# S4D long convolution on one core: undivided sums and state products, another order in every engine's slot, and Y's last table rows made by two engines

## The chip, the cores and the metric

One core of a Trainium2 chip. The metric is the device time of one execution in microseconds; lower is better.

## The reference

For each of 128 channels `h`, a real kernel `K[h, 0:2048]` is made of 64 complex exponentials, and every one of 64 sequences of 2048 samples is convolved with it causally; then come the skip term, the mask by length and the residual:

```python
A = -jnp.exp(log_A_real) + 1j * A_imag
dtA = A * dt[:, None]
P = dtA[:, :, None] * jnp.arange(length, dtype=jnp.float32)
Cs = Cc * (jnp.exp(dtA) - 1.0) / A
K = 2.0 * jnp.einsum('hn,hnl->hl', Cs, jnp.exp(P)).real
...
y = jnp.fft.irfft(u_f * k_f, n=n)[..., :Lq]
y = y + u_m * D[:, None]
return y * mask[:, None, :]          # and the result is x + this
```

x is float32 of 64 x 128 x 2048, so 64 MiB are read and 64 MiB written.

## The kernel before

No FFT is used. A sequence is cut into eight chunks of 256 samples, two halves of the sequence set side by side on the 128 partitions (64 sequences each). For one channel:

- TensorE transposes x in eight blocks of 128x128 (`turn_x`, parity 0 into `xt_even`, parity 1 into `xt_odd`), and the table E of the channel in two (`turn_e`).
- *Sums:* `even_sums` and `odd_sums`, three products of 448 columns each, bring each chunk into the state space (complex, 64 modes: real parts on one half of the partitions, imaginary on the other), in the PSUM bank `v`.
- *Scan:* VectorE carries the states from chunk to chunk: `pairs`, `fours`, `sixth`, `odds`, each as two dependent operations (the first into `mid`, the second into `v`). Multiplying by i needs the halves of the partitions swapped, which ScalarE does (`turn_odds`, `turn_pairs`, `turn_evens`, all into `turned`). The first operations of each are `fours_turned` and, after the change, `pairs_turned` and `odds_turned`.
- *Inside a chunk:* `toep_even` (three products each) and `toep_odd`, with the kernel's first 256 values as a Toeplitz matrix `traw` that SyncE loads with a DMA from `krows` in DRAM (`load_t`).
- *From the states:* `from_state`, twelve products of 256 columns with the scaled states `zhi`, `zlo` and the table F, into the bank `y`.
- *Choice and residual:* VectorE's `choose` copies `y` under the mask over x, in two halves of 512 columns; SyncE stores the result.

Products are fp32r with numbers split in a high part and a rest: ScalarE rounds the high part (`x_high`, `x_odd`, `e_high`, `f_high`, `t_high`, `z_high`), and VectorE or GpSimd subtracts it (`x_low`, `e_low`, `z_low` on VectorE; `f_low`, `t_low`, `odd_low` on GpSimd). GpSimd also makes E and F of a channel: two products of tables (16 x 16 each) and their `difference`.

The order on every engine is written out by hand: each has a `slot(g, j)` which handles stages of several channels (`here`, `one` ahead, `two` ahead, `three` ahead, `back`). `groups` runs it for channels 0 to 11 written out, for 12 to 119 in a hardware loop of 18 rounds of six, and for 120 to 127 written out. In TensorE's slot the even sums of the next channel come first, then the odd half of x two channels ahead, the odd sums, four Toeplitz steps with `turn_e` in the middle, and the products from the states, with the even half of x three channels ahead after the first six. Engines meet at semaphores, each counted up by one operation and waited for with the channel's number.

Ahead of the slots lies a prologue of some 60 us: VectorE and ScalarE compute powers of exp(dt A); GpSimd builds the table B by doubling (`level`, 1, 2, 4, 8 rows of 16), VectorE builds Y and then X, which needs the square root of a complex number (the norm on ScalarE, `m0`). TensorE transposes each four rows in the order of `STEPS` through three PSUM banks (`pro`), and ScalarE copies them to their place (`take`). B and X are doubled by a copy first (`double_b`, `double_x`). Then TensorE makes K (`k_fenced`, `k_rest`), which goes to `krows`. `keep_warm` are transposes without use.

## Time and profile before

| | |
|---|---|
| median of 3 runs | 887.85 us (887.10 to 889.97) |
| profiled execution | 887.13 us, span 885.3 us, mean granted clock 0.99 |
| busy | PE 829.4, VectorE (DVE) 758.5, ScalarE (ACT) 669.0, GpSimd (POOL) 605.6 us |
| DMA | 152.71 MB, 172 GB/s over the span |
| chain that ended last | PE 89%, DVE 4%, ACT 2%, DMA 2% |

A record of a row begins with its start from the start of the span and its duration, in us; the engine, the line, the operation, output<-input and their shapes follow, and in brackets the idle time of the engine ahead of it and who ended it. Records of one engine can overlap by the length of its pipeline.

### The profile page before, as it was taken

What the parts mean: (1) busy time and instruction counts of PE and PEld (TensorE: products, weight loads), DVE (VectorE), ACT (ScalarE), POOL (GpSimd) and SP (SyncE); (2) the same over time, 40 slices, a digit from 0 to 9 for tenths busy, and PEclk for the clock granted to TensorE, in tenths of its full rate; (3) what the DMA queues carried; (4) which work ended last, traced back from release to release, by engine and by line L of the source; (5) the groups of instructions that cost most, each with busy time, mean ns of one, the idle gap of its engine ahead of it and who ended that gap; (6) DMA issues with size and microseconds to landing.
All of it is one profiled execution on the core that took longest, in us unless ns stands there. A gap on an engine that the chain in (4) does not pass through costs nothing.

```text
span 885.3 us, 22927 instructions
## 1 busy us (share of the span) xinstructions
PE 829.4 (94%) x6281; PEld 788.1 (89%) x6281; DVE 758.5 (86%) x2041; ACT 669.0 (76%) x1720; POOL 605.6 (68%) x843
## 2 busy tenths in 40 slices
PE   0579999999999999999999999999999999999997
PEld 0569999999999999999999999999999999999996
DVE  7768888888888888888888888888888888888886
ACT  4567777777878787777777787878777777878784
POOL 5936767767676767676776767676767677676762
PEclk9789999999999999999999999999999999999999
DMA  5225787878877777877777778778787877778784
GB/s 104 48 61 115 175 194 177 187 186 186 186 184 190 180 191 175 190 178 192 180 187 184 185 186 182 191 180 188 178 189 179 190 181 185 184 186 186 185 191 107
DMA packets 161393, 152.71 MB, mean 172 GB/s; under 512 B 13656, under 2 KB 161240, under 8 KB 161240
## 3 DMA queue, kind: packets, MB, share of 16 engines
q1 hardware_dynamic: 161064, 152.15, 73.6%
q10 hardware_dynamic: 304, 0.26, 0.1%
q8 instruction: 11, 0.18, 0.1%
q14 instruction: 14, 0.11, 0.1%
HBM read 84.02 MB, written 67.30 MB: 171 GB/s over the span
## 4 chain that ended last, share of the span: by engine, by line
PE 89%; DVE 4%; issue 2%; ACT 2%; DMA 2%; SPq 0%; POOL 0%; DVEq 0%; ACTq 0%
PE y L1093 16%; PE y L1094 13%; PE y L1095 13%; PE y L1141 12%; PE xt_odd L1078 6%; PE xt_even L1078 6%; PE v L1093 6%; PE v L1094 6%; PE v L1095 6%; PE y L1088 2%; PE y L1089 2%; DMA xall<-in_x_dram 1%; ACT room L588 1%; PE y L1236 0%; ACT B L588 0%
## 5 line engine op out<-in xcount | busy, mean ns | idle before, releaser
L588 ACT ACTIVATE room<-v 64x192 f32<-64x192 f32 (+1 forms) x768 | 235.8, 307 | 153.3 <-DVE v L963 74.0
L963 DVE SCALAR_TENSOR_TENSOR mid<-room,RV,v 128x192 f32<-128x192 f32 (+2 forms) x512 | 183.1, 358 | 66.0 <-ACT room L588 58.9
L963 DVE SCALAR_TENSOR_TENSOR v<-v,RV,mid 128x192 f32<-128x192 f32 (+2 forms) x512 | 191.0, 373 | 38.6
L952 DVE COPY_PREDICATED xall<-mask,y 128x512 f32<-128x512 int32 x254 | 190.4, 750 | 0.5 <-issue 0.4
L1093 PE MATMUL y<-thi,uhi 128*128 128x256 f32 x511 | 175.9, 344 | 0.0
L1093 PE MATMUL y<-fhi,zhi 128*128 128x256 f32 x511 | 163.6, 320 | 12.7 <-DVE zlo L1008 1.2
L1095 PE MATMUL y<-fhi,zlo 128*128 128x256 f32 x511 | 144.3, 282 | 0.0
L1094 PE MATMUL y<-tlo,uhi 128*128 128x256 f32 x511 | 143.9, 282 | 0.0
L1094 PE MATMUL y<-flo,zhi 128*128 128x256 f32 x511 | 143.9, 282 | 0.0
L1095 PE MATMUL y<-thi,ulo 128*128 128x256 f32 x511 | 143.8, 281 | 0.0
L1141 PE MATMUL y<-traw,uod 128*128 128x128 f32 x680 | 130.5, 273 | 0.0
L1093 PEld LDWEIGHTS y<-fhi,zhi 128*128 128x128 f32 x511 | 96.7, 189 | 32.5 <-issue 32.5
L520 POOL TENSOR_TENSOR flo<-pf,fhi 128x256 fp32r<-128x256 f32 x64 | 46.6, 728 | 100.1 <-ACT fhi L588 100.1
L520 POOL TENSOR_TENSOR flo<-room,fhi 128x256 fp32r<-128x256 f32 x64 | 46.7, 729 | 96.2 <-ACT fhi L588 96.2
L557 POOL TENSOR_TENSOR uol<-uod,uoh 128x448 fp32r<-128x448 f32 x85 | 98.5, 1159 | 17.3 <-issue 14.1
L1141 PEld LDWEIGHTS y<-traw,uod 128*128 128x128 f32 x680 | 104.7, 190 | 0.0
L1093 PEld LDWEIGHTS y<-thi,uhi 128*128 128x128 f32 x511 | 97.4, 191 | 2.1
L1094 PEld LDWEIGHTS y<-tlo,uhi 128*128 128x128 f32 x511 | 97.8, 191 | 1.5
L1094 PEld LDWEIGHTS y<-flo,zhi 128*128 128x128 f32 x511 | 97.0, 190 | 0.0
L1095 PEld LDWEIGHTS y<-fhi,zlo 128*128 128x128 f32 x511 | 96.4, 189 | 0.0
L1095 PEld LDWEIGHTS y<-thi,ulo 128*128 128x128 f32 x511 | 96.1, 188 | 0.0
L525 POOL TENSOR_TENSOR tlo<-traw,thi 128x256 fp32r<-128x256 f32 x128 | 93.7, 732 | 0.3 <-ACT thi L588 0.3
(217 smaller groups left out, 2110.1 us busy)
## 6 DMA issues: line engine op xcount, KB each, us to landing
xall<-in_x_dram SPq DMA_DIRECT2D x256, 256.0 KB, 4.6
out_dram<-xall SPq DMA_DIRECT2D x254, 256.0 KB, 3.3
traw<-krows SPq DMA_DIRECT2D x128, 128.0 KB, 3.6
NXY<-B SPq DMA_DIRECT2D x2, 512.0 KB, 6.1
krows<-ksb SPq DMA_DIRECT2D x8, 1.0 KB, 2.2
krows<-ksb SPq DMA_DIRECT2D x8, 4.0 KB, 3.8
krows<-ksb SPq DMA_DIRECT2D x8, 11.0 KB, 4.0
out_dram<-xall SPq DMA_DIRECT2D x1, 128.0 KB, 2.5
```

The lines of the kernel that those rows point to most:

```text
L520: pool.tensor_tensor(flo[j % 2][:], pf[j % 2][:, ::-1], fhi[j % 2][:].bitcast(F32), ALU.subtract).then_inc(s_flo, 1)
L525: pool.tensor_tensor(tlo[j % 2][:], traw[j % 2][:, ::-1], thi[j % 2][:].bitcast(F32), ALU.subtract).then_inc(s_tlo, 1)
L557: pool.tensor_tensor(uol[j % 2][:], uod[j % 3][:, 0:EVERY], uoh[j % 2][:].bitcast(F32), ALU.subtract).then_inc(s_uol, 1)
L588: return act.activation(dst, src, ACT.Copy)
L952: dve.copy_predicated(xs[j][:, a:a + 512], mask[:, a:a + 512], yb[j % 2][part][:]).then_inc(s_pred, 1)
L963: return dve.scalar_tensor_tensor(out=out, in0=src, scalar=RV[:, k:k + 1, h], in1=other, op0=ALU.mult, op1=ALU.add)
L1078: mm = pe.transpose(xt[par][:, c * P:(c + 1) * P], xs[j][:, b * BLK:(b + 1) * BLK], ident[:])
L1088: pe.transpose(e_bank(j)[:, 0:P], pf[j % 2][:, 0:P], ident[:])
L1093: pe.matmul(o, a_hi, b_hi, start=start, stop=False, skip_group_check=True)
L1094: pe.matmul(o, a_hi, b_lo, start=False, stop=False, skip_group_check=True)
L1095: return pe.matmul(o, a_lo, b_hi, start=False, stop=stop, skip_group_check=True)
L1141: mm = pe.matmul(y_cols(g, j, c)[:, BLK:2 * BLK], uod[j % 3][:, b], traw[k][:, :BLK - 1:-1], start=False, stop=False, skip_group_check=True)
```

## The change

- TensorE's slot: even and odd sums of the next channel together; then all eight transposes of x two channels ahead; the products from the states undivided.
- VectorE's slot: both `choose` first; then the first operations of `odds` and of the next channel's `pairs`, then their second ones, `x_low`, `z_low`; `e_low`, `fours` and `sixth` of the next channel at the end.
- ScalarE's slot: `x_odd_high` (split off `x_odd`), `t_high` and `f_high` first; `x_high` and `x_odd` ahead of `z_high`.
- GpSimd's slot: the two table products apart, two channels ahead instead of three; `difference` last.
- SyncE: the load of x first in the slot and three channels ahead instead of four; the load of the Toeplitz matrix ahead of the store.
- Prologue: the square root right behind its squares and ahead of R's copies, an unused `Sqrt` earlier; B's last rows placed ahead of X's; the last eight rows of Y by GpSimd (four) and VectorE (four); B's last doubling by ScalarE instead of GpSimd; two more `keep_warm`; `fours` and `sixth` of channel 0 ahead of the slots.

```diff
--- before.py
+++ after.py
@@ -36,14 +36,14 @@
...
          ("B1", 12), ("B2", 12), ("Y1", 12), ("Y1", 8), ("B1", 8), ("B2", 8),
-         ("X1", 12), ("X2", 12), ("X1", 8), ("X2", 8), ("X1", 0), ("X1", 4), ("X2", 0), ("X2", 4),
-         ("B1", 0), ("B1", 4), ("B2", 0), ("B2", 4), ("Y1", 0), ("Y1", 4), ("S", 0)]
+         ("X1", 12), ("X2", 12), ("X1", 8), ("X2", 8), ("B1", 0), ("B1", 4), ("B2", 0), ("B2", 4),
+         ("X1", 0), ("X1", 4), ("X2", 0), ("X2", 4), ("Y1", 0), ("Y1", 4), ("S", 0)]
 T_K = len(STEPS)
...
 
-WARM, WARM_K = 16, 6
+WARM, WARM_B, WARM_Y = 16, 14, 4
 ROUND = 1.5 * 2.0 ** 23
...
@@ -279,10 +280,12 @@
...
-        def level(eng, link, table, turn, temps, k):
+        def level(eng, link, table, turn, temps, k, lo=0, hi=None):
 
             m = 2 ** k
-            old, new = slice(SQ - m, SQ), slice(SQ - 2 * m, SQ - m)
+            hi = m if hi is None else hi
+            old, new = slice(SQ - m + lo, SQ - m + hi), slice(SQ - 2 * m + lo, SQ - 2 * m + hi)
+            m = hi - lo
             re, im, re_new, im_new = table(old, 0), table(old, 1), table(new, 0), table(new, 1)
...
@@ -393,7 +396,7 @@
...
                 load_t(0, j)
-            tables_placed(sp, ("B2", 4))
+            tables_placed(sp, ("X2", 4))
             sp.dma_start(bsel[0:N], B1[0:N]).then_inc(s_bsel, 16)
...
@@ -403,6 +406,9 @@
...
                 early = isinstance(g, int) and g < 2
+                if exists(g, j, 3) and not (early and h + 3 < SLOTS):
+                    sp.wait_ge(s_out[(j + 3) % SLOTS], 32 * on(g, j, 3)[0])
+                    load_x(*on(g, j, 3))
                 if early and 2 <= h <= 5:
...
@@ -415,15 +421,12 @@
...
                     sp.wait_ge(s_kd_rest, 16 * 8)
+                if exists(g, j, 2):
+                    sp.wait_ge(s_intra, h + 1)
+                    load_t(*on(g, j, 2))
                 if exists(g, j, -1):
...
                     store(*on(g, j, -1))
-                if exists(g, j, 2):
-                    sp.wait_ge(s_intra, h + 1)
-                    load_t(*on(g, j, 2))
-                if exists(g, j, 4) and not (early and h + 4 < SLOTS):
-                    sp.wait_ge(s_out[(j + 4) % SLOTS], 32 * on(g, j, 4)[0])
-                    load_x(*on(g, j, 4))
             groups(sp, slot)
...
@@ -506,9 +509,9 @@
...
                 pool.wait_ge(s_nb, k)
-            late = slice(0, SQ // 2)
-            pool.tensor_copy(NB[:, late, 0, :], NB[:, late, 1, :]).then_inc(s_blate, 1)
-            pool.tensor_copy(NB[:, late, 3, :], NB[:, late, 2, :]).then_inc(s_blate, 1)
+            pool.wait_ge(s_ny, 2)
+            level(pool, link, lambda i, c: NXY[:, i, 1, c, :], (lre[:, A_POW + 3], lim[:, A_POW + 3]),
+                  [q1, q3, mag_flat, wide], 3, 0, 4).then_inc(s_ypool, 1)
             for n in range(2):
...
@@ -525,17 +528,14 @@
...
-            def table(g, j):
+            def product(g, j, which):
 
                 h = chan(g, j)
-                w1 = W1[:, 0, h, :].unsqueeze(2).broadcast_to([P, SQ, SQ])
-                w2 = W2[:, :, h].unsqueeze(2).broadcast_to([P, SQ, SQ])
-                b1 = B1[:, h, :].unsqueeze(1).broadcast_to([P, SQ, SQ])
-                b2 = B2[:, h, :].unsqueeze(1).broadcast_to([P, SQ, SQ])
-                if exists(g, j, -2):
+                w = (W1[:, 0, h, :], W2[:, :, h])[which].unsqueeze(2).broadcast_to([P, SQ, SQ])
+                b = (B1, B2)[which][:, h, :].unsqueeze(1).broadcast_to([P, SQ, SQ])
+                if which == 0 and exists(g, j, -2):
                     pool.wait_ge(s_pf, h - 1)
-                pool.tensor_tensor(tw1, w1, b1, ALU.mult).then_inc(s_gpa, 1)
-                pool.tensor_tensor(tw2, w2, b2, ALU.mult).then_inc(s_gpa, 1)
+                pool.tensor_tensor((tw1, tw2)[which], w, b, ALU.mult).then_inc(s_gpa, 1)
 
...
@@ -559,27 +559,24 @@
...
-                here, one, two, three = (g, j), on(g, j, 1), on(g, j, 2), on(g, j, 3)
-                has1, has2, has3 = exists(g, j, 1), exists(g, j, 2), exists(g, j, 3)
+                here, one, two = (g, j), on(g, j, 1), on(g, j, 2)
+                has1, has2 = exists(g, j, 1), exists(g, j, 2)
+                if has2:
+                    product(*two, 0)
                 f_low(*here)
-                if not exists(g, j, -1):
-                    t_low(*here)
-                if has2 and exists(g, j, -1):
-                    difference(*two)
                 if has1:
                     odd_low(*one)
-                if has2 and not exists(g, j, -1):
+                if has2:
+                    product(*two, 1)
+                t_low(*here)
+                if has2:
                     difference(*two)
-                if exists(g, j, -1):
-                    t_low(*here)
-                if has3:
-                    table(*three)
-
+
+            tables_placed(pool, ("X2", 4))
+            product(0, 1, 0)
+            product(0, 1, 1)
+            difference(0, 1)
             odd_low(0, 0)
-            tables_placed(pool, ("B2", 4))
-            table(0, 1)
-            difference(0, 1)
-            table(0, 2)
             groups(pool, slot)
...
@@ -594,6 +591,9 @@
...
                 copy(uod[j % 3][:], xt[1][:]).then_inc(s_uod, 1)
+
+            def x_odd_high(g, j):
+                act.wait_ge(s_tr, 2 * chan(g, j) + 2)
                 if exists(g, j, -2):
...
@@ -623,6 +623,8 @@
...
                            scale=-1.0).then_inc(s_sin, 1)
+            act.wait_ge(s_pool0, 1)
+            act.activation(one_root[:], pw[:, 0:1], ACT.Sqrt)
             act.wait_ge(s_lam, 2)
...
@@ -646,32 +648,35 @@
...
-            take(("R", 0), ("R", 1))
             act.wait_ge(s_z, 1)
...
             act.activation(sq_im, z_im, ACT.Square).then_inc(s_sq, 1)
+            act.wait_ge(s_n2, 1)
+            act.activation(m0, n2, ACT.Sqrt).then_inc(s_m0, 1)
+            take(("R", 0), ("R", 1))
             act.wait_ge(s_nb, 1)
             double_b(slice(12, 16))
-            take(("B1", 12), ("Y1", 12))
-            act.wait_ge(s_n2, 1)
-            act.activation(m0, n2, ACT.Sqrt).then_inc(s_m0, 1)
             x_high(0, 0)
             x_odd(0, 0)
-            take(("Y1", 8), ("Y1", 8))
+            take(("B1", 12), ("Y1", 12))
+            x_odd_high(0, 0)
             act.wait_ge(s_nb, 2)
             double_b(slice(8, 12))
-            take(("B1", 8), ("B2", 8))
+            take(("Y1", 8), ("B2", 8))
             act.wait_ge(s_nx, 1)
...
             take(("X1", 8), ("X2", 8))
+            act.wait_ge(s_nb, 3)
+            double_b(slice(0, SQ // 2))
+            take(("B1", 0), ("B2", 4))
             act.wait_ge(s_nx, 3)
             double_x(slice(0, SQ // 2))
-            take(("X1", 0), ("B2", 4))
+            take(("X1", 0), ("X2", 4))
             act.wait_ge(s_ny, 3)
-            tables_placed(act, ("B2", 4))
+            tables_placed(act, ("X2", 4))
             copy(b0[:, 0], B1[:, 0, :])
...
@@ -730,22 +735,24 @@
...
                 has0, has1, has2 = exists(g, j, 0), exists(g, j, 1), exists(g, j, 2)
-                three, has3 = on(g, j, 3), exists(g, j, 3)
+                if has1:
+                    x_odd_high(*one)
+                t_high(*here)
+                if has1:
+                    f_high(*one)
                 turn_evens(*here)
...
                         k_copy(j)
-                    t_high(*one)
+                if has2:
+                    x_high(*two)
+                    x_odd(*two)
                 z_high(*here)
                 if has1:
-                    f_high(*one)
                     turn_pairs(*one)
...
                     e_high(*two)
-                    x_odd(*two)
-                if has3:
-                    x_high(*three)
 
...
@@ -755,8 +762,6 @@
...
             turn_pairs(0, 0)
-            t_high(0, 0)
-            x_high(0, 2)
             groups(act, slot)
...
@@ -911,7 +916,7 @@
...
             dve.wait_ge(s_ny, 2)
-            level(dve, link, y_table, coarse[3], temps, 3).then_inc(s_ny, 1)
+            level(dve, link, y_table, coarse[3], temps, 3, 4, 8).then_inc(s_ny, 1)
 
...
@@ -963,11 +968,15 @@
...
-            def pairs(g, j):
-
-                h, z, m, w = chan(g, j), chunks(vb[j % 2]), mid[j % 2], turned[j % 2]
+            def pairs_turned(g, j):
+
+                h, z, m, w = scan(g, j)
                 dve.wait_ge(s_turn1, h + 1)
                 times(m[:], w[:, 0:3], h, 1, z[:, 2:7:2]).then_inc(s_mid1, 1)
+
+            def pairs(g, j):
+
+                h, z, m, w = scan(g, j)
                 dve.wait_ge(s_mid1, h + 1)
...
@@ -995,11 +1004,15 @@
...
-            def odds(g, j):
-
-                h, z, m, w = chan(g, j), chunks(vb[j % 2]), mid[j % 2], turned[j % 2]
+            def odds_turned(g, j):
+
+                h, z, m, w = scan(g, j)
                 dve.wait_ge(s_turn4, h + 1)
                 times(m[:], w[:, 0:3], h, 1, z[:, 3:8:2]).then_inc(s_mid4, 1)
+
+            def odds(g, j):
+
+                h, z, m, w = scan(g, j)
                 dve.wait_ge(s_mid4, h + 1)
...
@@ -1013,29 +1026,27 @@
...
                 has0, has1, has2, hasb = exists(g, j, 0), exists(g, j, 1), exists(g, j, 2), exists(g, j, -1)
-                if has1:
-                    e_low(*one)
-                fours(*here)
-                if hasb and has1:
-                    dve.wait_ge(s_y, 2 * h - 1)
-                    choose(*back, 0)
-                sixth(*here)
-                if hasb and has1:
-                    dve.wait_ge(s_y, 2 * h)
-                    choose(*back, 1)
-                odds(*here)
-                if hasb and not has1:
+                if hasb:
                     dve.wait_ge(s_y, 2 * h - 1)
...
                     choose(*back, 1)
+                odds_turned(*here)
+                if has1:
+                    pairs_turned(*one)
+                odds(*here)
                 if has1:
                     pairs(*one)
-                z_low(*here)
                 if has2:
                     x_low(*two)
+                z_low(*here)
                 if has1:
                     fours_turned(*one)
+                if has2:
+                    e_low(*two)
+                if has1:
+                    fours(*one)
+                    sixth(*one)
                 if isinstance(g, int) and g == 0 and j == 1:
...
@@ -1044,14 +1055,18 @@
...
             dve.wait_ge(s_b0, 1)
-            tables_placed(dve, ("B2", 4))
+            tables_placed(dve, ("X2", 4))
             first_table()
...
             x_low(0, 1)
+            pairs_turned(0, 0)
             pairs(0, 0)
+            e_low(0, 1)
             fours_turned(0, 0)
+            fours(0, 0)
+            sixth(0, 0)
             dve.wait_ge(s_mask, 2)
...
@@ -1062,10 +1077,12 @@
...
-            def keep_warm(n, bank):
-
+            def keep_warm(n, t):
+
+                if t >= BANKS:
+                    pe.wait_ge(s_free[t % BANKS], t // BANKS)
                 for _ in range(n):
-                    pe.transpose(bank[:, 0:P], ident[:], ident[:])
+                    pe.transpose(pro[t % BANKS][:, 0:P], ident[:], ident[:])
 
...
@@ -1160,10 +1177,10 @@
...
                     even_sums(*one)
+                    odd_sums(*one)
                 if has2:
+                    turn_x(*two, 0)
                     turn_x(*two, 1)
-                if has1:
-                    odd_sums(*one)
                 if isinstance(g, int) and g == 0 and 1 <= j <= 4:
...
@@ -1177,11 +1194,7 @@
...
                     toep_odd(*here, c)
-                for c in range(2):
-                    from_state(*here, c)
-                if exists(g, j, 3):
-                    turn_x(*on(g, j, 3), 0)
-                for c in range(2, CPH):
+                for c in range(CPH):
                     from_state(*here, c)
...
@@ -1240,7 +1253,7 @@
...
             turn_x(0, 0, 1)
-            keep_warm(WARM, pro[BANKS - 1])
+            keep_warm(WARM, STEPS.index(("B1", 12)))
             pe.wait_ge(s_bdup, 1)
...
@@ -1254,16 +1267,18 @@
...
                 turn(("X2", i), ("X2", i))
+            keep_warm(WARM_B, STEPS.index(("B1", 0)))
+            pe.wait_ge(s_bdup, 3)
+            turn(("B1", 0), ("B2", 4))
             pe.wait_ge(s_nx, 3)
...
             turn(("X2", 0), ("X2", 4))
-            pe.wait_ge(s_blate, 1)
-            turn(("B1", 0), ("B1", 4))
-            pe.wait_ge(s_blate, 2)
-            turn(("B2", 0), ("B2", 4))
+            keep_warm(WARM_Y, STEPS.index(("Y1", 0)))
+            pe.wait_ge(s_ypool, 1)
+            turn(("Y1", 0), ("Y1", 0))
             pe.wait_ge(s_ny, 3)
-            turn(("Y1", 0), ("Y1", 4))
+            turn(("Y1", 4), ("Y1", 4))
             tables_placed(pe, ("Y1", 4))
...
@@ -1274,7 +1289,6 @@
...
             turn_e(0, 1)
-            turn_x(0, 2, 0)
             tables_placed(pe, ("S", 0))
...
```

## Rows read from the trace of the kernel before

**Rows 1.** The page: busy us of each engine (share of the span) xinstructions.

```profile
PE 829.4 (94%) x6281; PEld 788.1 (89%) x6281; DVE 758.5 (86%) x2041; ACT 669.0 (76%) x1720; POOL 605.6 (68%) x843
```

**Rows 2.** Windows: stretch, length, busy time of each engine, granted clock, DMA, GB/s.

```profile
70.00:100.00 30.00, 30.00 (x242) 29.43 (x242) 24.99 (x67) 23.50 (x62) 19.45 (x27) 1.00 0.62 145
```

**Rows 3.** Timeline of TensorE (PE), a slot and a bit of the loop.

```profile
401.58 0.39 PE L1141 MATMUL y<-traw,room 128*128 128x128 f32 x2
402.07 0.36 PE L1093 MATMUL y<-fhi,zhi 128*128 128x256 f32 x1
402.26 0.28 PE L1094 MATMUL y<-flo,zhi 128*128 128x256 f32 x1
...
405.47 0.36 PE L1095 MATMUL v<-uoh,elo 128*128 128x448 f32 x1
...
408.46 0.35 PE L1093 MATMUL y<-fhi,zhi 128*128 128x256 f32 x1
```

**Rows 4.** Timeline, SyncE's queue (SPq), two channels written out near the end.

```profile
855.59 0.33 SPq L373 DMA_DIRECT2D traw<-krows  x1
...
861.87 0.33 SPq L373 DMA_DIRECT2D traw<-krows  x1
```

**Rows 5.** Timeline of VectorE (DVE), the same stretch of the loop.

```profile
406.67 0.41 DVE L963 SCALAR_TENSOR_TENSOR mid<-room,RV,v 128x192 f32<-128x192 f32 x1 [0.43 <-ACT room L588]
407.22 0.43 DVE L963 SCALAR_TENSOR_TENSOR v<-v,RV,mid 128x192 f32<-128x192 f32 x1
407.63 0.68 DVE L1008 SCALAR_TENSOR_TENSOR zlo<-v,RV,zhi 128x448 fp32r<-128x448 f32 x1
408.24 0.68 DVE L775 TENSOR_TENSOR ulo<-xt_even,uhi 128x512 fp32r<-128x512 f32 x1
408.83 0.33 DVE L963 SCALAR_TENSOR_TENSOR mid<-room,RV,v 128x128 f32<-128x128 f32 x1
409.09 0.41 DVE L775 TENSOR_TENSOR elo<-y,ehi 128x256 fp32r<-128x256 f32 x1
...
409.69 0.75 DVE L952 COPY_PREDICATED xall<-mask,y 128x512 f32<-128x512 int32 x1
```

**Rows 6.** Timeline of ScalarE (ACT), the same stretch of the loop.

```profile
405.86 0.66 ACT L588 ACTIVATE room<-v 64x192 f32<-64x192 f32 x2 [0.53 <-PE v L1095]
...
406.87 0.62 ACT L727 ACTIVATE zhi<-v,RV 128x448 fp32r<-128x448 f32 x1
...
409.16 0.55 ACT L588 ACTIVATE uoh<-xt_odd 128x448 fp32r<-128x448 f32 x1
```

**Rows 7.** The chain that ended last: start, us, what; one group of transposes.

```profile
74.88 0.44 PE xt_even L1078 x4
```

**Rows 8.** Timeline of the prologue, all engines.

```profile
19.51 0.39 ACT L588 ACTIVATE y<-lre 128x256 f32<-128x256 f32 x1 [2.14 <-DVE lre L866]
...
26.43 0.78 DVE L896 SCALAR_TENSOR_TENSOR root<-root 128x64 f32<-128x64 f32 x1 [2.25 <-ACT root L652]
...
31.21 1.28 ACT L657 ACT_TABLE_LOAD   x1
...
32.79 0.55 DVE L902 RECIPROCAL root<-root 128x64 f32<-128x64 f32 x1 [3.37 <-ACT root L657]
...
36.33 1.26 POOL L299 TENSOR_TENSOR room<-xall 128x512 f32<-128x512 f32 x1
...
36.38 1.30 DVE L908 TENSOR_TENSOR NXY<-root 128x64 f32<-128x64 f32 x1
...
46.97 1.09 ACT L588 ACTIVATE W<-v 128x512 f32<-128x512 f32 x2
...
52.89 0.46 PE L1222 MATMUL y<-B,W 64*128 64x128 f32 x2 [1.50 <-ACT W L641]
```

**Rows 9.** Timeline of GpSimd (POOL), the same stretch of the loop.

```profile
409.84 1.16 POOL L557 TENSOR_TENSOR uol<-room,uoh 128x448 fp32r<-128x448 f32 x1 [0.16 <-issue]
```

**Rows 10.** DMA issues by tile: count, KB each, median us from issue to landing.

```profile
xall<-in_x_dram SPq DMA_DIRECT2D x256, 256.0 KB, 4.6
```

More of the change, by code:

```diff
@@ L183, in s4d_kernel @@
         s_n2 = sem("s_n2")
+        s_ypool = sem("s_ypool")
         s_m0 = sem("s_m0")
```

2 lines of the change are left out of this document (1 added, 1 removed).

## The prediction

> **What bounds the kernel now.** I read the page first: TensorE is busy for 94% of the span [rows 1], so either its own work or something that it waits for sets the end. The split into windows separates the two. Between 70 and 100 us TensorE has no idle time at all [rows 2]. Later, in the loop, the timeline shows one slot (one channel) every 6.39 us: the first product from the states starts at 402.07 and the next at 408.46 [rows 3]. That stretch is not pure work. The last Toeplitz product starts at 401.58 and ends at 401.97. Its next neighbour should end 0.12 us later, as products of 256 columns do here, but ends at 402.43: TensorE stands for 0.34 us. So its own work in a slot is 6.39 - 0.34 = 6.05 us. The 0.34 us are lost 108 times in the loop (channels 12 to 119). The slots that are written out before and after it run at 861.87 - 855.59 = 6.28 us [rows 4].
>
> What ends that wait is VectorE's `z_low`, seen one slot later: it starts at 407.63 [rows 5], ends at 408.31, and TensorE's product starts at 408.46. Following it back closes a ring: the last odd sum ends at 405.47 + 0.36 = 405.83 [rows 3]; ScalarE turns the halves at 405.86 to 406.52 [rows 6]; VectorE's `pairs` start at 406.67 and 407.22, and `z_low` at 407.63 [rows 5]; then TensorE does the products from the states, one group of four transposes (0.44 us, [rows 7]) in their middle, the even sums, a second group of four between the two halves of the sums, and the odd sums. The ring is 1.80 us off TensorE (405.83 to 407.63) and 4.59 us from there to the next end of the odd sums. It is this ring, and no engine's busy share, that is 6.39 us long.
>
> **The change part by part.** *TensorE's slot.* The same instructions in another order: both halves of the sums first, then all eight transposes of the next channel, then the Toeplitz products, then the twelve products from the states undivided. Work stays at 6.05 us. In the ring, the transposes lay between `z_low` and the end of the odd sums; now they lie behind the sums, beside the work of ScalarE and VectorE. The ring loses 2 x 0.44 = 0.88 us on its TensorE side.
>
> *The other side of the ring gets longer*, since VectorE now puts its work between. From the end of the odd sums: ScalarE's turn 0.03 + 0.66 (as 405.83 to 406.52), the step to VectorE 0.15 (406.52 to 406.67), then `pairs_turned`, `odds`, `pairs` and `x_low` ahead of `z_low`. In unbroken flow VectorE starts the next instruction about 0.07 us before the last one's record ends (408.83 + 0.33 against 409.09, [rows 5]), so these take 0.41 - 0.07 = 0.34, 0.43 - 0.07 = 0.36 twice, and 0.60 (407.63 to 408.24, same width class as `x_low`). Sum 0.69 + 0.15 + 0.34 + 0.72 + 0.60 = 2.50 us against 1.80 before. The second road to `z_low` goes over ScalarE: it turns, then copies `x_high` and `x_odd` (two copies of 512 columns lie 0.49 us apart, as 1.09 - 0.60 in [rows 8]), then `z_high` 0.62 [rows 6] and the step of 0.15: 0.69 + 0.03 + 0.98 + 0.62 + 0.15 = 2.47 us. Both arrive together. New ring: 6.39 - 0.88 + (2.50 - 1.80) = 6.21 us; with the few hundredths of uncertainty of each overlap I take 6.20. That is above TensorE's 6.05, so the ring still decides and a stall of about 0.15 us remains ahead of the products from the states. Gain in the loop: 108 x 0.19 = 20.5, taken between 108 x 0.14 and 108 x 0.24.
>
> The written-out slots have the same ring at 6.28; it drops by the same 0.18 to 6.10, near the floor of 6.05. Slots 1 to 4 also hold K's products on TensorE and have no stall, so they keep their time. Some 13 slots x 0.19 = 2.5 us.
>
> *What is moved past what, and what hides it.* VectorE takes both `choose` copies at the head of the slot, behind the end of the products from the states of the channel before. They take 0.75 us each [rows 5]. The first can start at about the slot's start, so `odds_turned` can follow at 1.4 us and has to be out by 2.2, when the turned halves of the sums arrive: 0.4 us of cover are left after it. If that cover went, every further 0.1 us would cost 13 us in all. Queued behind these waits are `odds`, `pairs` and `z_low`, for which TensorE waits. ScalarE's `f_high` goes to the head of its slot and waits for the last product from the states; behind it stand `turn_evens` and `turn_odds`. It ends 0.6 us into the slot, `turn_evens` at 1.3, and the odd sums' end comes at 1.4: cover 0.1 us only, and this is the thinnest place of the ring. `f_low` on GpSimd is then done a slot early, which ends its long waits for ScalarE at no gain, as the ring did not go through it. `x_odd_high` moves to the slot's head (0.55 us, [rows 6]); GpSimd's `odd_low` behind it takes 1.16 us [rows 9] and has to be ready for the odd sums: 5.1 + 0.15 + 1.16 = 6.4 us after the slot's start against 6.8 needed, 0.4 us of cover. Its two table products and the difference are spread around it; no one waits for them within 2 us.
>
> *SyncE's queue.* x is asked for three channels ahead instead of four, but at the head of the slot: right behind the store before, and no longer behind the wait for the Toeplitz products. The loads go out at about 6.4 us after a slot's start, and the transposes that want them come 7.2 us later. Landing takes 4.6 us in the median [rows 10]. Stores wait behind that same wait now; the next user of their slot comes three slots on. I cost both at nothing; 2.6 us of cover.
>
> *The prologue.* The root: ScalarE's `Sqrt` comes only after three table copies, with a table load of 1.28 us before it [rows 8], and VectorE idles 3.37 us for it. Now a dummy `Sqrt` loads the table in ScalarE's idle 2.14 us before 19.51 [rows 8], and the squares go ahead of R's copies, so that the norm follows the first Y levels at about 24.3 rather than 26.43 [rows 8]. Behind it stand 0.8 us for the norm and 2.1 us for a Y level, so VectorE reaches the reciprocal at 27.2 instead of 32.79: 5.6 us. The steps of the root then go on oddly slowly, 1.30 us for 64 columns at 36.38, ending with GpSimd's operation of 36.33 to 37.59 [rows 8]; four of them each wait for such an end. At 27.2 GpSimd is in its shorter level (0.7 us an operation), and the last wait falls into the long level, so the root ends at about 31.4, not 37.7: 6.3 us for X. Half of Y's last level (8 rows, now 4) goes to GpSimd at 37.7 to 41.9. Next late is ScalarE: B's last level is GpSimd's and ends at 37.6 as before; then its doubling (1.1, now ScalarE's), four copies of B, doubling X 0.6, four of X, two small ones 0.3, two of Y, at 0.55 each: 37.7 + 1.1 + 5.5 + 0.9 + 0.7 for hand-overs and cold transposes = 45.9 at the best, 49 at the worst. I take 47.4 for the first product of K, which was at 52.89 [rows 8]: 5.5 us, between 4 and 7.
>
> The Trainium skill, "ScalarE: Activation LUTs", section "What ACT_TABLE_LOAD costs", speaks against this part: it counts 1.28 us for the load and as much again for a drain. No row here shows the second half: the square root follows its load at once. By the page the dummy would overrun its gap by about 0.5 us, and the total would be 0.5 us longer.
>
> *Start-up* of the first channels: `e_low` of channel 1 no longer stands behind a wait for turned halves; 0.9 us earlier, less 0.4 for the four transposes that used to be done in idle time: 0.5. *End:* `choose` now stands ahead of the last `odds`: 0.3 us lost.
>
> **Sum.** 20.5 + 2.5 + 5.5 + 0.5 - 0.3 = 28.7 us. The profiled execution took 887.13 us (its span 885.3), 0.7 below the median of 887.85. 887.13 - 28.7 = 858.4, or 859 on the scale of the median.
>
> **The rivals.** (a) *The ring closes below TensorE's work*, 0.62 for the forecast, 0.14 for this one: if both roads to `z_low` are 0.15 shorter, every slot runs at 6.05. 108 x 0.34 + 13 x 0.23 + 5.7 = 45: 843 us. For it: 70 to 100 us without idle time; against it: the two roads agree with each other within 0.03. (b) *The ring shrinks by less*, 0.19: an instruction that had to wait starts its follower late (406.67 to 407.22 is 0.55 for a record of 0.41, [rows 5]). If `odds` and `pairs` each behave like that (up to 0.14 more), or ScalarE's `f_high` makes the turn late by 0.1, a slot takes 6.30 to 6.39: 866 to 878 us. For it is that very row; against it, that this follower waits for its forerunner's result, which `odds` no longer does. (c) *Slower*, 0.05: the x loads. With three channels of lead, a burst of 128 KB, two stores and two loads goes out in 3.3 us. If the pair then lands more than 7.2 us after its issue, TensorE waits for it at the transposes; the slot is then half of (5.1 + landing), and from a landing of 7.7 us on it is above 6.39. At 8.3 us: 6.70 a slot, 120 x 0.31 = 37 us lost less 6 of the prologue: 919 us. Against it: 4.6 us now.
>
> **How the numbers follow.** Likeliest 859, its own range 851 to 866. The bound from both sides is 6.05 (843) and 6.39 (878); 844 to 873 leaves out the upper half of (b), (c) and some of (a). Under 0.3% a run of this kernel tells nothing. All cases but (c) are faster: 0.94; the same 0.02; slower 0.04.
>
> **What would show it.** Right: a slot of about 6.2 in the loop, TensorE's wait ahead of the products from the states still there but near 0.15 us and released by `z_low`; all transposes without a wait; the reciprocal of the root near 27, the first product of K near 47. Wrong: waits of TensorE at the transposes with a DMA as releaser (c), at the odd sums with GpSimd as releaser, slots at 6.05 with no wait (a), or `turn_odds` starting later than 0.1 us after the sums (b).

## The result, and the profile after

The changed kernel takes 862.51 us (median of 4, 860.40 to 864.69) against 888.37 us of the kernel before in the same measurement: ratio 0.9708, 95% interval 0.9672 to 0.9744, 25.9 us less. 859 us were predicted. The profiled execution took 864.69 us, its span is 862.8 us; the span of before is 885.3. The four executions differ in their granted clock: the two with a mean of 0.999 took 860.40 and 860.65 us, the two with 0.996 took 864.37 and 864.69, so a profile can lie 4 us from its fellows.

Here are the line of the page that answers to [rows 1], and behind it the windows' row for 100 us in the loop (stretch, length, busy time of each engine with the number of instructions, granted clock, DMA share, GB/s):

```profile
PE 821.8 (95%) x6299; PEld 787.6 (91%) x6299; DVE 743.1 (86%) x2041; ACT 674.4 (78%) x1722; POOL 603.6 (70%) x847
```

```profile
400.00:500.00 100.00, 100.00 (x771) 96.11 (x771) 88.05 (x243) 80.85 (x209) 71.78 (x97) 1.00 0.70 189
```

TensorE now reads 100% busy. That is not its peak: a record of a product reaches over the end of the one before, and a wait of 0.2 us disappears in that. The timeline shows it, TensorE in one slot of the loop (answers to [rows 3]):

```profile
403.41 0.39 PE L1158 MATMUL y<-traw,uod 128*128 128x128 f32 x2
...
403.74 0.36 PE L1110 MATMUL y<-fhi,zhi 128*128 128x256 f32 x1
...
403.94 0.28 PE L1111 MATMUL y<-flo,zhi 128*128 128x256 f32 x1
...
406.26 0.37 PE L1112 MATMUL v<-uoh,elo 128*128 128x448 f32 x1
...
409.97 0.36 PE L1110 MATMUL y<-fhi,zhi 128*128 128x256 f32 x1
```

From 403.74 to 409.97 a slot takes 6.23 us, where [rows 3] have 6.39. The last Toeplitz product ends at 403.41 + 0.39 = 403.80, the first product from the states at 404.10; 0.12 us would do, so 0.18 us of wait are left of 0.34. The ring can be read off the timelines of VectorE and ScalarE (they answer to [rows 5] and [rows 6]):

```profile
407.47 0.41 DVE L968 SCALAR_TENSOR_TENSOR mid<-room,RV,v 128x192 f32<-128x192 f32 x1 [0.48 <-ACT room L585]
...
407.80 0.74 DVE L968 SCALAR_TENSOR_TENSOR v<-v,RV,mid 128x192 f32<-128x192 f32 x2
...
408.46 0.68 DVE L780 TENSOR_TENSOR ulo<-xt_even,uhi 128x512 fp32r<-128x512 f32 x1
...
409.13 0.69 DVE L1021 SCALAR_TENSOR_TENSOR zlo<-v,RV,zhi 128x448 fp32r<-128x448 f32 x1
```

```profile
405.89 1.44 ACT L585 ACTIVATE room<-v 64x192 f32<-64x192 f32 x4
...
408.36 0.64 ACT L732 ACTIVATE zhi<-v,RV 128x448 fp32r<-128x448 f32 x1
```

The odd sums end at 406.26 + 0.37 = 406.63. ScalarE's four half turns (two of `turn_evens`, two of `turn_odds`) end at 407.33, `pairs_turned` starts at 407.47, `odds` and `pairs` at 407.80 (x2), `x_low` at 408.46, `z_low` at 409.13: 2.50 us from the end of the sums, where 2.50 were worked out. `z_high` ends at 409.00 and its step of 0.13 ends at the same moment: both roads meet, as forecast.

In the prologue, ScalarE, VectorE and TensorE (they answer to [rows 8]):

```profile
17.40 1.28 ACT L627 ACT_TABLE_LOAD   x1
...
18.69 0.20 ACT L627 ACTIVATE one_root<-pw 128x1 f32<-128x1 f32 x1
...
26.59 0.55 DVE L907 RECIPROCAL root<-root 128x64 f32<-128x64 f32 x1
...
29.48 0.76 DVE L913 TENSOR_TENSOR NXY<-root 128x64 f32<-128x64 f32 x1
...
46.84 0.46 PE L1235 MATMUL y<-B,W 64*128 64x128 f32 x2 [1.30 <-ACT W L643]
```

The table load lies in ScalarE's gap, the reciprocal starts 6.2 us earlier (26.59 against 32.79), and the first product of K 6.05 us earlier (46.84 against 52.89).

### The profile page after: what moved, and what is told of

It reads as the page before. It is cut to its first block, busy times and chain, and to the rows that moved or that the text cites. A ratio compares the mean times of both kernels' runs of the same rounds, so it can differ in the third digit from the quotient of the medians.

```text
span 862.8 us, 23096 instructions
## 1 busy us (share of the span) xinstructions
PE 821.8 (95%) x6299; PEld 787.6 (91%) x6299; DVE 743.1 (86%) x2041; ACT 674.4 (78%) x1722; POOL 603.6 (70%) x847
## 4 chain that ended last, share of the span: by engine, by line
PE 88%; ACT 3%; DMA 3%; DVE 3%; SPq 1%; issue 1%; POOL 0%; DVEq 0%; ACTq 0%; POOLq 0%
PE y L1110 15%; PE y L1111 13%; PE y L1112 13%; PE y L1158 12%; PE xt_even L1095 6%; PE xt_odd L1095 6%; PE v L1110 6%; PE v L1112 6%; PE v L1111 6%; DMA xall<-in_x_dram 3%; PE y L1105 2%; PE y L1106 2%; SPq L369 1%; ACT B L585 0%; DVE zlo L1021 0%
## 5 line engine op out<-in xcount | busy, mean ns | idle before, releaser
L968 DVE SCALAR_TENSOR_TENSOR mid<-room,RV,v 128x192 f32<-128x192 f32 (+2 forms) x512 | 185.1, 361 | 73.8 <-ACT room L585 55.9
L968 DVE SCALAR_TENSOR_TENSOR v<-v,RV,mid 128x192 f32<-128x192 f32 (+2 forms) x512 | 177.7, 370 | 16.5
L1110 PE MATMUL y<-thi,uhi 128*128 128x256 f32 x511 | 186.4, 365 | 0.0
L957 DVE COPY_PREDICATED xall<-mask,y 128x512 f32<-128x512 int32 x254 | 178.2, 752 | 1.4 <-issue 1.3
L538 POOL TENSOR_TENSOR room<-W,B 128x256 f32 (+1 forms) x254 | 161.8, 637 | 23.5 <-POOL room L547 11.1
L1110 PE MATMUL y<-fhi,zhi 128*128 128x256 f32 x511 | 153.7, 301 | 3.2 <-DVE zlo L1021 3.2
L557 POOL TENSOR_TENSOR uol<-room,uoh 128x448 fp32r<-128x448 f32 x43 | 49.7, 1157 | 68.5 <-issue 68.0
```

Of the source, the lines that this page charges most:

```text
L538: pool.tensor_tensor((tw1, tw2)[which], w, b, ALU.mult).then_inc(s_gpa, 1)
L557: pool.tensor_tensor(uol[j % 2][:], uod[j % 3][:, 0:EVERY], uoh[j % 2][:].bitcast(F32), ALU.subtract).then_inc(s_uol, 1)
L957: dve.copy_predicated(xs[j][:, a:a + 512], mask[:, a:a + 512], yb[j % 2][part][:]).then_inc(s_pred, 1)
L968: return dve.scalar_tensor_tensor(out=out, in0=src, scalar=RV[:, k:k + 1, h], in1=other, op0=ALU.mult, op1=ALU.add)
L1110: pe.matmul(o, a_hi, b_hi, start=start, stop=False, skip_group_check=True)
```

## The experiments

Every kernel was timed in rounds against the kernel before on its own chip; what is compared are the ratios to it, since that kernel's median went from 888 to 891 us between chips. The figure of a slot is the distance of SyncE's Toeplitz loads, one each channel, in the profiled execution.

**e1: the prologue alone.** The kernel before with the changed order of `STEPS`, the root, B and Y (the diff's parts in the prologue, word for word), and the slots of before.

```diff
-         ("X1", 12), ("X2", 12), ("X1", 8), ("X2", 8), ("X1", 0), ("X1", 4), ("X2", 0), ("X2", 4),
-         ("B1", 0), ("B1", 4), ("B2", 0), ("B2", 4), ("Y1", 0), ("Y1", 4), ("S", 0)]
+         ("X1", 12), ("X2", 12), ("X1", 8), ("X2", 8), ("B1", 0), ("B1", 4), ("B2", 0), ("B2", 4),
+         ("X1", 0), ("X1", 4), ("X2", 0), ("X2", 4), ("Y1", 0), ("Y1", 4), ("S", 0)]
```

> The kernel before with the prologue of the change alone (root behind its squares, B's last rows ahead of X's, Y's last rows by two engines), slots as before. My theory (5.5 us from the prologue, the rest from the ring of the slots): 882 to 883 us, first product of K at about 47, slots of the loop still 6.39 us, three slots with K's products still 6.97. Rival, that the prologue's gain is given back before the loop begins (the changed kernel is only 4.0 us ahead at channel 10 although 6.05 ahead at the first product of K): 884 to 885, and the slots 1 to 4 would then be longer here too.

Measured: 881.43 us against 890.97, ratio 0.9900 (0.9881 to 0.9918): 8.9 us by the medians' ratio, 7.3 to 10.6. The profiled spans say 6.9 (878.4 against 885.3), but 885.3 is from another chip and from the fastest execution of the kernel before there; on e1's own chip its spans are 887.6 to 890.5. The first product of K comes 6.7 us earlier:

```profile
46.20 0.46 PE L1231 MATMUL y<-B,W 64*128 64x128 f32 x2 [1.30 <-ACT W L646]
...
401.18 0.34 SPq L376 DMA_DIRECT2D traw<-krows  x1
...
407.58 0.35 SPq L376 DMA_DIRECT2D traw<-krows  x1
```

Slots of the loop are 6.40 us, those with K's products 6.97, as before. So the prologue's gain is carried to the end whole here, and the slots with K's products don't take any of it back, as they do in the changed kernel. 882 to 883 was a little too high; the gain is 6.7 us or more, not 5.5.

**e2: the ring made longer without more work.**

```diff
 even_sums(*one)
-odd_sums(*one)
 if has2:
     turn_x(*two, 0)
+if has1:
+    odd_sums(*one)
+if has2:
     turn_x(*two, 1)
```

> The changed kernel with four of the eight transposes put back between the even and the odd sums; TensorE's work is the same. Theory of the ring (z_low, products from the states, sums, turned halves, z_low): all 0.44 us enter the ring, a slot of the loop takes 6.23 + 0.43 = 6.66 us, with the written-out slots some 50 us more: about 912 us. Rival, that TensorE's own work sets the slot of the changed kernel (its busy share reads 100%): no change, 862. Between them, if another wait than z_low's ended last: 870 to 890.

Measured: 914.28 us, ratio 1.0261 (1.0243 to 1.0280). The changed kernel has 0.9708 and 0.9693 in its two measurements, so 0.053 to 0.057 lie between, 49 us. The waits of TensorE (total, times, longest) and SyncE's loads:

```profile
PE y L1110 <- DVE zlo L1021: 46.2, 127, 0.7
```

```profile
403.62 0.35 SPq L376 DMA_DIRECT2D traw<-krows  x1
...
410.28 0.34 SPq L376 DMA_DIRECT2D traw<-krows  x1
```

A slot takes 6.66 us, 0.43 more, and the wait that grew is the one for `z_low`, seen 127 times. Four transposes of 0.44 us in total, put to where the ring passes, cost the whole of their time; where the changed kernel has them, beside the scan, they cost nothing. So TensorE's own work was not the bound.

**e3: the copy of K last in ScalarE's slot.** `k_copy`, four times in the first slots, moved from behind `turn_odds` to behind `e_high`.

```diff
     turn_odds(*one)
-    if isinstance(g, int) and g == 0 and 1 <= j <= 4:
-        k_copy(j)
...
 if has2:
     e_high(*two)
+if isinstance(g, int) and g == 0 and 1 <= j <= 4:
+    k_copy(j)
```

> The changed kernel with ScalarE's copy of K (k_copy, slots 1 to 4) moved from behind turn_odds to the end of its slot. The slots 1 to 3 of the changed kernel take 7.3 to 7.65 us against 6.97 before. Theory: the copy, which waits for TensorE's products of K, holds up x_high, x_odd and z_high, and so z_low: moved away, these slots go back to about 7.0 and the kernel gains 1.5 to 2 us: 860.5 to 861. Rival: they are longer for another reason (the transposes of the next x have lost their cover, or a DMA): no change.

Measured: 861.92 us, ratio 0.9669 (0.9647 to 0.9691), so 0.4% less than the changed kernel's 0.9708, but the intervals overlap. The slots decide. SyncE's loads for channels 4 to 6 in the kernel before, in the changed one and here:

```profile
81.12 0.36 SPq L373 DMA_DIRECT2D traw<-krows  x1
...
88.09 0.36 SPq L373 DMA_DIRECT2D traw<-krows  x1
...
94.84 0.36 SPq L373 DMA_DIRECT2D traw<-krows  x1
```

```profile
76.47 0.36 SPq L376 DMA_DIRECT2D traw<-krows  x1
...
84.12 0.36 SPq L376 DMA_DIRECT2D traw<-krows  x1
...
91.55 0.36 SPq L376 DMA_DIRECT2D traw<-krows  x1
```

```profile
75.10 0.36 SPq L376 DMA_DIRECT2D traw<-krows  x1
...
82.05 0.36 SPq L376 DMA_DIRECT2D traw<-krows  x1
...
88.78 0.36 SPq L376 DMA_DIRECT2D traw<-krows  x1
```

That is 6.97 and 6.75 us before, 7.65 and 7.43 changed, 6.95 and 6.73 here. The slot ahead of these is longer by 0.7 us too, the one behind them by 0.6: from channel 2's load to channel 7's it is 33.63 us before, 36.32 changed and 33.62 here, so the copy costs 2.7 us in four slots. ScalarE and TensorE in the changed kernel show how:

```profile
81.59 0.60 ACT L585 ACTIVATE ksb<-y 128x512 f32<-128x512 f32 x1 [1.10 <-PE y L1249]
...
83.04 0.65 ACT L732 ACTIVATE zhi<-v,RV 128x448 fp32r<-128x448 f32 x1
```

```profile
84.56 0.36 PE L1110 MATMUL y<-fhi,zhi 128*128 128x256 f32 x1 [0.47 <-DVE zlo L1021]
```

ScalarE stands 1.10 us for K's products, since TensorE makes them behind the transposes now, and `x_high`, `x_odd` and `z_high` come after the copy; TensorE then stands 0.47 us for `z_low`. The 2.7 us won, more than the 1.5 to 2 expected, are shown by the slots. The total shows less, and in the profile there is a reason: TensorE waits for x five times here, 3.5 us in all, against four times and 1.7 us in the changed kernel's.

**e4: the root alone put back.** ScalarE's order in the changed kernel, with the root and its squares behind the same copies as before, and without the early `Sqrt`.

```diff
-act.wait_ge(s_pool0, 1)
-act.activation(one_root[:], pw[:, 0:1], ACT.Sqrt)
...
+take(("R", 0), ("R", 1))
 act.wait_ge(s_z, 1)
 act.activation(sq_re, z_re, ACT.Square)
 act.activation(sq_im, z_im, ACT.Square).then_inc(s_sq, 1)
-act.wait_ge(s_n2, 1)
-act.activation(m0, n2, ACT.Sqrt).then_inc(s_m0, 1)
-take(("R", 0), ("R", 1))
 act.wait_ge(s_nb, 1)
 double_b(slice(12, 16))
+take(("B1", 12), ("Y1", 12))
+act.wait_ge(s_n2, 1)
+act.activation(m0, n2, ACT.Sqrt).then_inc(s_m0, 1)
 x_high(0, 0)
 x_odd(0, 0)
-take(("B1", 12), ("Y1", 12))
```

> The changed kernel with the square root alone put back: no early table load, squares behind R's copies, the root behind the copies of B and Y. Theory: X is ready 6 to 7 us later (near 45), and since B's rows are placed ahead of X's, half of ScalarE's work behind it is already done: first product of K at 50 to 51 instead of 46.84, so 3.5 to 4.5 us more: about 866.5. Rival, that the reordering of B and Y makes the gain and the root was hidden by GpSimd's B: less than 1 us more.

Measured: 871.75 us, ratio 0.9782 (0.9763 to 0.9802), 6.6 us more than the changed kernel (0.9708), not 4. VectorE and TensorE:

```profile
32.93 0.55 DVE L905 RECIPROCAL root<-root 128x64 f32<-128x64 f32 x1 [3.44 <-ACT root L657]
...
53.34 0.46 PE L1233 MATMUL y<-B,W 64*128 64x128 f32 x2 [1.30 <-ACT W L641]
```

With the root late, the first product of K comes at 53.34, later than in the kernel before (52.89). The other order of B, X and Y alone gains nothing: without the early root nothing of the prologue's gain is left. Whether the root alone, in the old order, would bring all of it was not run. That the order of B would save half of ScalarE's work even so was wrong.

**e5 and e6: the changed kernel again, and SyncE's slot as before the change** (store, Toeplitz load, load of x four channels ahead).

```diff
-if exists(g, j, 3) and not (early and h + 3 < SLOTS):
-    sp.wait_ge(s_out[(j + 3) % SLOTS], 32 * on(g, j, 3)[0])
-    load_x(*on(g, j, 3))
-if exists(g, j, 2):
-    sp.wait_ge(s_intra, h + 1)
-    load_t(*on(g, j, 2))
...
+if exists(g, j, 2):
+    sp.wait_ge(s_intra, h + 1)
+    load_t(*on(g, j, 2))
+if exists(g, j, 4) and not (early and h + 4 < SLOTS):
+    sp.wait_ge(s_out[(j + 4) % SLOTS], 32 * on(g, j, 4)[0])
+    load_x(*on(g, j, 4))
```

> The changed kernel itself once more, as the measure for the three others of this chip: ratio to the kernel before 0.970 to 0.973, slots of the loop 6.23 us.

> The changed kernel with SyncE's slot as before: store, Toeplitz load, then the load of x four channels ahead. TensorE waited for x five times in the changed kernel's profile (0.5 to 0.7 us each with what follows), once or twice before. Theory: with TensorE's transposes of x now in one block at the slot's head, it is the lead that matters; four channels ahead, but behind the store's wait, gives the loads about 5 us less or more of time depending on the queue: within 0.3% of the changed kernel, and at most 2 us faster if these waits come from the three-channel lead. Rival (c) of the prediction: if the shorter lead costs, this kernel is clearly faster, by 3 us or more.

Measured: e5 862.74 us, ratio 0.9693 (0.9672 to 0.9714); e6 862.58 us, 0.9684 (0.9661 to 0.9707). The totals differ by less than their intervals. In the profiles there is a difference: TensorE waits for x three times in e5 (total in us, times, longest), and never in e6.

```profile
PE xt_even L1095 <- DMA xall<-in_x_dram: 1.6, 3, 0.7
```

**e7: the ring cut.** VectorE does `odds` before `pairs`, and `z_low` before `x_low`; ScalarE `z_high` before `x_high` and `x_odd`.

```diff
 odds_turned(*here)
+odds(*here)
 if has1:
     pairs_turned(*one)
-odds(*here)
-if has1:
     pairs(*one)
+z_low(*here)
 if has2:
     x_low(*two)
-z_low(*here)
```

> The changed kernel with the ring cut shorter: VectorE does both operations of odds before pairs, and z_low ahead of x_low; ScalarE does z_high ahead of x_high and x_odd. Theory of the ring: z_low then starts about 3.3 us after the sums begin instead of 3.89, TensorE's wait ahead of the products from the states (0.18 us) is gone, and a slot takes TensorE's own 6.05 us: 108 x 0.18 = 19 us less in the loop, 843 us where the changed kernel has 862. Rival: VectorE itself is the next bound, as two dependent operations side by side wait 0.14 us twice and it has some 5.9 us of work a slot: 6.1 to 6.2 us a slot, 848 to 860.

Measured: 886.13 us, ratio 0.9956 (0.9940 to 0.9971). Neither expectation held. In the loop the wait ahead of the products from the states is gone, and another has come ahead of the odd sums. ScalarE, GpSimd and TensorE in one slot:

```profile
404.77 0.56 ACT L585 ACTIVATE room<-v 64x128 f32<-64x128 f32 x2
...
405.63 0.54 ACT L585 ACTIVATE uoh<-xt_odd 128x448 fp32r<-128x448 f32 x1
...
406.30 1.16 POOL L557 TENSOR_TENSOR uol<-room,uoh 128x448 fp32r<-128x448 f32 x1 [1.71 <-issue]
...
407.15 0.36 PE L1111 MATMUL v<-uhi,elo 128*128 128x448 f32 x1
...
407.61 0.44 PE L1109 MATMUL v<-uoh,ehi 128*128 128x448 f32 x1
```

The next product starts 0.46 us behind the one of 407.15, where 0.20 us is normal. GpSimd's `odd_low` starts at 406.30 and ends at 407.46, behind ScalarE's `x_odd_high` (405.63 to 406.17); that stands behind `turn_pairs` and `e_high`, and these were moved back by the time that ScalarE now stands idle ahead of `z_high` (0.37 us in this slot). A slot takes 6.39 us, and every sixth 6.8.

**e8: e7 and the copy of K last.**

> As e7, and the copy of K at the end of ScalarE's slot as in e3. Theory: both gains add, 1.5 to 2 us less than e7. Rival: with z_high ahead of x_high the copy of K holds up nothing that TensorE waits for, except that it waits for it: within 1 us of e7.

Measured: 882.78 us, 0.9916 (0.9896 to 0.9936): 0.4% or 3.6 us less than e7, clear of the intervals and more than the 1.5 to 2 us expected; by the slots with K's products it is 2.5 us. The copy's cost adds on, as in e3.

**e9: `x_odd_high` right behind `x_odd`,** else as e7.

```diff
-if has1:
-    x_odd_high(*one)
 t_high(*here)
...
 x_odd(*two)
+x_odd_high(*two)
```

> e7 was slow, 6.39 us a slot and 6.8 every sixth: TensorE's wait ahead of the products from the states had gone, but a wait ahead of the odd sums had come, released by GpSimd's odd_low, whose x_odd_high stood behind ScalarE's turn_pairs and e_high. Here x_odd_high follows x_odd directly, all else as e7. Theory: that wait goes; but turn_pairs is 0.42 us later, VectorE already waited 0.28 us for it, so VectorE's own order becomes the ring: 6.2 to 6.4 us a slot, 860 to 882. Rival, that only GpSimd held it up: 6.05 us a slot, 843.

Measured: 936.92 us, ratio 1.0538 (1.0515 to 1.0561), far outside. ScalarE and VectorE:

```profile
399.42 0.64 ACT L732 ACTIVATE zhi<-v,RV 128x448 fp32r<-128x448 f32 x1 [0.81 <-DVE v L968]
...
400.90 0.56 ACT L585 ACTIVATE uoh<-xt_odd 128x448 fp32r<-128x448 f32 x1
...
401.49 0.56 ACT L585 ACTIVATE room<-v 64x128 f32<-64x128 f32 x2
...
402.18 0.35 DVE L968 SCALAR_TENSOR_TENSOR mid<-room,RV,v 128x128 f32<-128x128 f32 x1 [0.71 <-ACT room L585]
```

`turn_pairs` comes 0.59 us behind the start of `x_odd_high`, and VectorE stands 0.71 us for it. A slot is 6.83 us. The expectation named VectorE's order as the next ring, but with 6.2 to 6.4 us a slot it expected a kernel faster than e7; its ratio is 0.058 above e7's. The rows show another ring, over VectorE and ScalarE alone: VectorE's two `choose` and `odds`, for which `z_high` waits 0.81 us, then ScalarE's `x_high`, `x_odd`, `x_odd_high` and `turn_pairs`, for which VectorE waits, then `fours` and `sixth`, and behind them the next two `choose`.

**e10: an order that serves all three rings.** VectorE as in e7 and `fours` ahead of `e_low`; ScalarE's slot against the changed kernel:

```diff
-if has1:
-    x_odd_high(*one)
 t_high(*here)
...
     x_high(*two)
-    x_odd(*two)
 z_high(*here)
 if has1:
     turn_pairs(*one)
 if has2:
+    x_odd(*two)
+    x_odd_high(*two)
     e_high(*two)
```

> z_low early without ScalarE standing idle: VectorE as in e7, and fours ahead of e_low; ScalarE in the order turn_evens, turn_odds, x_high, z_high, turn_pairs, x_odd, x_odd_high, e_high, t_high, f_high. By the rows of the changed kernel z_low starts 3.4 us after the sums (needed at 3.7), the rest of the odd half of x is ready at 6.3 (needed at 6.5), E's rest at 5.9 (needed at 6.0), and VectorE is full with about 6.05 us. Theory of the rings: 6.05 to 6.12 us a slot, 843 to 850. Rival, VectorE's work and its own waits are more than that: 6.2 or more, 860.

Measured: 848.18 us, ratio 0.9534 (0.9518 to 0.9550). The windows' row of the same 100 us:

```profile
400.00:500.00 100.00, 100.00 (x793) 97.51 (x792) 90.07 (x247) 82.67 (x215) 73.31 (x100) 1.00 0.72 195
```

There are 793 products against 771 in the changed kernel, and a slot takes 6.07 us: TensorE's own work, 0.02 above the 6.05 worked out from before. Every sixth slot, at the loop's branch, takes 6.25. VectorE, the next in line, is busy for 90% of that stretch.

**e11 and e12: e10 with SyncE's slot as before the change (the edit of e6), and e11 with the copy of K last as well (the edit of e3).**

> As e10, with the copy of K last in ScalarE's slot (e3) and SyncE's slot as before the change (e6, which had no wait of TensorE for x). Theory: 2 us less than e10 for the copy and 1 to 2 us less for the missing waits: 840 to 847. Rival: at 6.05 us a slot the DMA queues are fuller, the waits for x come with either order: as e10 less 2.

> e10 with SyncE's slot as before the change and nothing else. e11, with the copy of K moved too, was 5 us faster than e10, of which e3's slots explain 2. Theory: the rest is SyncE's order, TensorE's waits for x (1.6 us by the waits of e10, more by the slots behind them) go: ratio to the kernel before 0.950, 2.5 to 3 us less than e10. Rival: the copy of K weighs more in the short slots, 3 us or more, and SyncE's order nothing, as in e6: ratio 0.953.

Measured: e11 843.05 us, ratio 0.9478 (0.9463 to 0.9494); e12 845.15 us, 0.9485 (0.9466 to 0.9503). SyncE's order by itself (e12 against e10) is worth 0.5%, 4.4 us, by the ratios; the two were measured on different chips, and two of e12's five executions had a granted clock of 0.998 and 1.0, where e10's had 0.995 to 0.997. The profiled spans (845.5 and 843.1, clocks 0.995 and 0.996) are 2.4 us apart, which fits the 2.5 to 3 expected. In e10 TensorE waited for x, in e12 it did not:

```profile
PE xt_even L1095 <- DMA xall<-in_x_dram: 1.6, 3, 0.8
```

The three waits stand in slots of 7.10, 6.58 and 6.78 us, 2.3 us above 6.07 together, which is nearly all of those 2.4. The copy of K (e11 against e12) is 0.1%, within the intervals; by the four slots behind channel 3's load (28.1 us in e12, 26.7 in e11; one of them 7.34 against 6.96) it is 1.4 us. e11 is the fastest kernel of this study, 5.2% below the kernel before.

## Why the prediction was right, and where it was off

The mechanism of the loop came out, and its term is the largest; by the medians the sum is 2.8 us too high, by the spans 6.2. The terms from the first product of K to channel 5 missed by 3.9 together, the loop by 3.2, and the first product of K and the end gave 1.5 back. The table holds the terms of the sum against the profiled executions. Their spans differ by 22.5 us, the medians by 25.9, and 28.7 were predicted: before's profiled execution was the fastest of its four, the changed kernel's the slowest.

| step | predicted | measured |
|---|---|---|
| first product of K | 5.5 earlier | 6.05 (e1: 6.7) |
| from there to the end of channel 0's Toeplitz products | 0.5 gained | 0.7 lost (e2: 1.3 gained) |
| channels 1 to 5 (K's products on TensorE) | 0 | 2.7 lost |
| loop, 108 slots, with their waits for x (0.5 lost, net) | 0.19 each, 20.5 | 0.16 each, 17.3 |
| written-out slots | 2.5 | 2.4 |
| waits for x outside the loop | 0 | 0.6 lost, net |
| end | 0.3 lost | 0.7 gained |

- **The ring** was right in mechanism, and in price to 0.03 us a slot. Both of its sides came out to 0.01 us in the slot shown: 2.50 us off TensorE, and 3.72 us on it (409.13 back to 402.91 is a slot of 6.22, less 2.50) against 4.59 - 0.88 = 3.71. That it is this ring which sets the slot is shown by e2 and, in the other direction, by e10. The sum gave 6.21, so a gain of 0.18; "I take 6.20" made it 0.19, which is 1.1 us in all without a reason. The measured slot is 6.23, another 0.02 a slot or 2.2 us.
- **Rival (a)**, slots at TensorE's work, did not come about but is what e10 reaches. **Rival (b)**, late followers of an operation that waited, was not seen: `odds` starts 0.33 us behind `pairs_turned`, in unbroken flow.
- **Rival (c)**, x late with three channels of lead, was given 0.05 as a catastrophe and happens as a trifle: single waits of 0.3 to 0.8 us. "Cost at nothing; 2.6 us of cover" was wrong in the lead. The loads were to stand 7.2 us ahead of their transposes; SyncE issues them after the two stores, and the first stands 6.4 us ahead and the second, which the transposes wait for as well, some 5.5; the sign "all transposes without a wait" did not hold either:

```profile
406.32 1.49 SPq L364 DMA_DIRECT2D xall<-in_x_dram  x2
```

```profile
412.70 0.60 PE L1095 MATMUL xt_even<-ident,xall 128*128 128x128 f32 x4
```

  Landing takes 4.3 us in the median of the 256 loads and 7.0 at most, so a cover of 1.2 us is left for the second load and none for the slowest. In e6 the lead is 8.2 us (409.63 to 417.80), landing takes 6.9 at most, and no wait is left. Next to a slot of 6.23 the order can't be told in the total (e6); next to one of 6.07 it is 2.4 us in the spans, 4.4 by the ratios (e12 against e10).
- **"Slots 1 to 4 keep their time"** is a step that failed. The prediction took from [rows 2] that TensorE had no idle time there, and did not follow where ScalarE's copy of K stands once the transposes lie ahead of K's products. Four slots are 0.6 to 0.7 us longer, 2.7 in all; shown by e3.
- **The start-up** was argued from `e_low` alone. The odd sums of channel 1 then wait for GpSimd's `odd_low`, and behind that wait the same product of 448 columns lasts 0.57 us against 0.36, and the transposes and first Toeplitz products are longer as well until 60.3:

```profile
53.20 0.36 PE L1111 MATMUL v<-ulo,ehi 128*128 128x448 f32 x1
...
54.98 0.71 PE L1110 MATMUL v<-uoh,ehi 128*128 128x448 f32 x1 [1.21 <-POOL uol L557]
...
55.49 0.57 PE L1111 MATMUL v<-uol,ehi 128*128 128x448 f32 x1
```

  The wait itself doesn't explain the 0.7 us lost. In e2's profile, with the same work up to there but for the place of four transposes, the odd sums also wait for `odd_low`, but the granted clock stays at 1.00 (50 to 64 us), and from the first product of K to the end of channel 0's Toeplitz products 1.3 us are gained (13.06 us against 14.37 before; 15.06 in the changed kernel's profile). The difference of 2.0 us goes with the clock:

```profile
54.65 0.37 PE L1111 MATMUL v<-uol,ehi 128*128 128x448 f32 x1
```

- **The prologue** was costed about right, 5.5 against 6.05, with two errors inside. The root was to end at 31.4 and ended at 30.24, since its last operation (29.48) still fell beside a short one of GpSimd, so X began 7.4 us earlier and not 6.3; and ScalarE's doubling of B began at 38.60, not 37.7. e4 shows that nothing of the gain is left without the early root. The Trainium skill, "ScalarE: Activation LUTs", "What ACT_TABLE_LOAD costs", counts a drain of about the load's own length on top of each load. The trace doesn't show it: the load of 17.40 ends at 18.68 and the dummy root runs at 18.69; the copies behind it, at 19.56, wait for VectorE. The measurement decides. The root's operations again last as long as GpSimd's beside them: 0.76 us for 64 columns at 29.48, beside one of 0.73, where the same instruction took 1.30 beside one of 1.26 [rows 8]. The Trainium skill, "GPSIMD Engine Reference", "Key points", says that GpSimd shares its SBUF interfaces with VectorE, with contention when a VectorE instruction has two SBUF inputs; these numbers agree with it.

Left open: why the granted clock falls at the start of the slots in some executions and not in others, and how much of the spread between executions of one kernel (spans 4.4 us apart in e5 and 3.5 in e12, shorter with the higher clock) is its doing.

## What to carry to other kernels

When no engine is idle and none is full, follow one wait back until it comes round to itself, and count a slot as the length of that ring; moving work of the busiest engine out of the ring takes all of its time off it, less what the other engines then put in (0.88 us less 0.70 here), and moving it in costs all of it (49 us here for 0.44 us a slot). After each cut ask for the next ring, through every engine's own order: two cuts that looked as good as the one that worked (e7, e9) cost the changed kernel 0.025 and 0.083 of the time of before, as each made a short copy on ScalarE come some tenths of a microsecond too late. And the few special slots at the start need their own look: an instruction that sits in only four of them stood in the ring.

## What was not expected of the hardware

- A TensorE row at 100.00 busy hides a wait of 0.18 us in every slot (771 products in 100 us against 793 in e10): the number of instructions in a window tells more than the busy time.
- At the start of the slots TensorE's granted clock fell once more in the changed kernel's profile, and did not in e2's. It stood without work for 1.21 us ahead of the product of 54.98, and the next of the same 448 columns took 0.57 us where the one of 53.20 took 0.36. The windows' rows have a granted clock of 0.84 from 56 to 70 us, a mean over stretches at the two levels (1.2 and 2.4 GHz), and then 1.00. In the kernel before it was 0.81 between 56 and 70 us.

```profile
56.00:70.00 14.00, 13.54 (x94) 13.10 (x93) 9.06 (x23) 9.41 (x24) 6.62 (x11) 0.84 0.15 32
70.00:90.00 20.00, 19.07 (x151) 18.22 (x150) 15.18 (x42) 13.79 (x37) 13.29 (x18) 1.00 0.53 144
```

- In the hardware loop the slot at the branch, every sixth, was 0.2 us longer once TensorE alone set the pace (6.25 against 6.07), and 0.4 us longer where rings over the other engines did (6.8 against 6.39 in e7, 7.26 against 6.83 in e9). In the changed kernel, with a wait of 0.18 us in each slot, it doesn't show.
